# Statistics, scaling, delta pieces and softplus at other places in the queues, and the small scan kept in PSUM

## What is computed

```python
x = x + mamba(cond_scan(x))     # _L0_attn_ref(_L0_cond_ref(x, ...), ...)
x = x + bitlinear_ffn(lowrank_layer(x, cond))
```

## Time and profile before

| | |
|---|---|
| median of 3 runs | 2885.6 us (2884.72 to 2888.72) |
| the profiled execution | 2885.02 us, span 2883.0 us |
| PE busy, DVE busy | 2396.6 us, 2378.5 us |
| ACT busy, POOL busy | 1675.9 us, 1682.5 us |
| mean granted TensorE clock | 0.916 of full speed |
| first and last large scan start | 114.0 us, 2359.3 us |

### The profile page before, as it was taken

How to read it: one execution, slowest core, us unless ns; L and a number is a source line. 1 busy time by engine, 2 the same in 40 slices (tenths; PEclk the granted TensorE clock), 3 DMA queues, 4 the chain that set the end, 5 groups by cost and what they waited for, 6 DMA issues and landing times. The chain is left out here.

```text
span 2883.0 us, 38176 instructions
## 1 busy us (share of the span) xinstructions
PE 2396.6 (83%) x11520; PEld 1642.8 (57%) x11520; DVE 2378.5 (83%) x2438; ACT 1675.9 (58%) x3282; POOL 1682.5 (58%) x1993
## 2 busy tenths in 40 slices
PE   7878878788878888888888888888888794899997
PEld 5556656565656565666665666565656331444443
DVE  2489898898898988898888898898989664688887
ACT  2565656565757565657575656565656444555654
POOL 0266667676767676767676767676767550222221
PEclk8888999998999898999999999999988896999999
DMA  4101010201020201010110101010102531121110
GB/s 171 66 2 68 7 70 5 71 5 70 5 71 5 74 13 63 16 59 31 45 51 24 60 16 60 15 63 13 60 8 89 205 139 71 55 66 55 65 59 23
DMA packets 47510, 152.50 MB, mean 53 GB/s; under 512 B 7973, under 2 KB 8869, under 8 KB 44206
## 3 DMA queue, kind: packets, MB, share of 16 engines
q1 hardware_dynamic: 47278, 149.76, 14.4%
HBM read 132.37 MB, written 17.37 MB: 52 GB/s over the span
## 5 line engine op out<-in xcount | busy, mean ns | idle before, releaser
L451 POOL TENSOR_TENSOR ring<-ring,Cbc 128x512 f32<-128x512 f32 x1024 | 1292.1, 1283 | 44.2
L841 DVE TENSOR_TENSOR_SCAN ring<-a_ps,ring 128x1024 f32<-128x1024 f32 x512 | 1165.2, 2278 | 50.8 <-ACT a_ps L658 50.4
L658 ACT ACTIVATE a_ps<-delta,nA 128x255 f32<-128x255 f32 x2048 | 851.0, 465 | 452.7 <-DVE ring L841 450.5
L1038 PE MATMUL yT_ps<-ident,ring 128*128 128x128 f32 x4096 | 606.4, 291 | 234.4 <-POOL ring L451 224.3
L1038 PEld LDWEIGHTS yT_ps<-ident,ring 128*128 128x128 f32 x4096 | 486.5, 148 | 360.2 <-POOL ring L451 315.2
L833 DVE TENSOR_TENSOR ring<-u_ps,Bbc 128x1024 f32<-128x1024 f32 x512 | 619.9, 1211 | 45.0 <-PE yT_ps L1038 38.9
L1004 PE MATMUL work<-xb,big 128*128 128x256 f32 x2048 | 487.0, 394 | 0.0
L444 POOL TENSOR_TENSOR carry<-ring,half 128x4 f32<-128x4 f32 x512 | 146.5, 286 | 581.7 <-DVE ring L841 579.3
L1004 PEld LDWEIGHTS work<-xb,big 128*128 128x128 f32 x2048 | 398.7, 200 | 54.3 <-issue 0.4
L977 PE MATMUL work<-y0s,big 128*128 128x256 f32 x1024 | 243.6, 396 | 0.7 <-issue 0.7
L1020 PE MATMUL work<-Wout,xb 128*128 128x512 f32 x512 | 239.5, 606 | 0.0
(11 more groups left out here) (194 smaller groups left out, 2697.4 us busy)
## 6 DMA issues: line engine op xcount, KB each, us to landing
Bbc<-bc_rows SPq DMA_DIRECT2D x64, 512.0 KB, 4.5
Cbc<-bc_rows SPq DMA_DIRECT2D x64, 512.0 KB, 3.9
xT<-in_xT SPq DMA_DIRECT2D x16, 514.0 KB, 3.3
x_rows<-x2row SPq DMA_DIRECT2D x32, 256.0 KB, 2.0
xp<-x_rows SPq DMA_DIRECT2D x32, 256.0 KB, 2.7
xx<-in_x SPq DMA_DIRECT2D x32, 256.0 KB, 3.0
out_rows<-orow SPq DMA_DIRECT2D x32, 256.0 KB, 2.0
delta<-in_c_w SPq DMA_DIRECT2D x6, 1024.0 KB, 4.9
```

Source lines behind the costliest of these rows:

```text
L451: nc.gpsimd.tensor_tensor(hp, hp, Cbc[:, G * g + GP * c:G * g + GP * c + GP, :], ALU.mult)\
L658: r = nc.scalar.activation(a_ps[q % 2][:, i, 1:T], delta[:, par, dt, 1:T], ACT.Exp, scale=nA[:, dt, s:s + 1])
L841: dve.tensor_tensor_scan(ring[:, q % RING, :, :].rearrange("p g t -> p (g t)"), a_ps[q % 2][:, :, :].rearrange("p g t -> p (g t)"), ring[: ...
L1038: r = pe.matmul(yT_ps[:, tt, :], ring[:, q % RING, i, P * tt:P * tt + P], ident[:, :], is_transpose=True, start=False, stop=(g == NG - 1 a ...
```

## The change

On DVE, the small scan writes its result over its input in PSUM (bank 0) and no longer to st0; the carry and y0 are read from there. The bank is released one step later: after y0, by a memset that waits for it. A new semaphore, s_sc0, takes the place of the bank's own for the wait on the scan. On DVE the statistics 0 go from slot 7 to 6, the late minimum from slot 4 to 3, the late maximum from slot 6 to 7. On ACT, y0's scaling and copy back, the copies of x and z, zsilu, dexp and dln and the first-column exponential get other slots. On PE, WO1 goes from slot 8 to slot 6, x and z each go about a slot later, and the last two quarters of delta's projection are spread over slots 24 to 31. Nothing is left out and nothing added but the semaphore and the memset.

```diff
@@ -180,6 +180,7 @@
         s_tanh = sem("s_tanh")
         s_l0 = sem("s_l0")
         s_c0 = sem("s_c0")
+        s_sc0 = sem("s_sc0")
         s_y0k = sem("s_y0k")
         s_stat = sem("s_stat")
         s_rstd = sem("s_rstd")
@@ -609,19 +610,19 @@
                     nc.scalar.activation(xw[:, c % 2, :], work[0][0:2, :], ACT.Copy).then_inc(s_rowcp, 1)
 
 
-                next_plan = {5: [prj], 6: [prj_ln], 10: [y0scale], 11: [y0back], 14: [lambda: xcopy(0)],
-                             15: [lambda: xcopy(1)], 16: [lambda: xcopy(2)], 17: [lambda: xcopy(3), silu],
-                             18: [lambda: zcopy(0), lambda: zcopy(1)], 19: [lambda: zcopy(2), lambda: zcopy(3)],
-                             21: [zsilu], 22: [bc], 24: [lambda: dexp(0, False)], 25: [lambda: dexp(1, False)],
-                             26: [lambda: dln(0, False)], 32: [lambda: dexp(2, False)]}
-                scan_plan = {3: [lambda: dexp(3, True)], 6: [lambda: dln(1, True)]}
-                turned = {13: 0, 20: 1, 28: 2}
+                next_plan = {5: [prj], 6: [prj_ln], 12: [y0scale], 13: [y0back], 15: [lambda: xcopy(0)],
+                             16: [lambda: xcopy(1)], 17: [lambda: xcopy(2)], 18: [lambda: xcopy(3), silu],
+                             19: [lambda: zcopy(0)], 20: [lambda: zcopy(1), lambda: zcopy(2)], 21: [lambda: zcopy(3)],
+                             22: [bc], 23: [zsilu], 24: [lambda: dexp(0, False)], 26: [lambda: dexp(1, False)],
+                             27: [lambda: dln(0, False)], 30: [lambda: dexp(2, False)]}
+                scan_plan = {1: [lambda: dexp(3, True)], 6: [lambda: dln(1, True)]}
+                turned = {14: 0, 21: 1, 28: 2}
                 back_plan = {6: [lambda: gT(ND // 2 - 1, fp)], 9: [lambda: wout(0)], 11: [lambda: wout(1)]}
                 for q in range(NQ + 1):
                     dt, g = q // NG, q % NG
-                    if scan and q == FIRST[1] + 2:
+                    if scan and q == FIRST[1] + 3:
                         first_exp(1, k)
-                    if front and q == FIRST[0] + 2:
+                    if front and q == FIRST[0] + 3:
                         first_exp(0, k + 1)
                     if isinstance(k, int) and k == -1 and q == 13:
                         mz_copy()
@@ -717,13 +718,15 @@
                     dve.scalar_tensor_tensor(ps[0:N0, T:2 * T], ps[0:N0, T:2 * T], V[0:N0, V_BS:V_BS + 1], e0[:, :],
                                              ALU.add, ALU.mult).then_inc(s_c0, 1)
                     dve.wait_ge(s_c0, base + 3)
-                    dve.tensor_tensor_scan(st0[:, :], sc0[0:N0, 3:4].to_broadcast([N0, T]), ps[0:N0, T:2 * T],
-                                           carry0[:, fp:fp + 1], ALU.mult, ALU.add).then_inc(free[BANK["PRJ"]], 1)
-                    dve.wait_ge(free[BANK["PRJ"]], jobs_before("PRJ", k) + 1)
-                    dve.tensor_copy(carry0[:, fp:fp + 1], st0[:, T - 1:T]).then_inc(s_c0, 1)
-
-                    dve.scalar_tensor_tensor(y0[0:N0, :], st0[:, :], sc0[0:N0, 1:2], c0[:, :],
+                    dve.tensor_tensor_scan(ps[0:N0, T:2 * T], sc0[0:N0, 3:4].to_broadcast([N0, T]), ps[0:N0, T:2 * T],
+                                           carry0[:, fp:fp + 1], ALU.mult, ALU.add).then_inc(s_sc0, 1)
+                    dve.wait_ge(s_sc0, n + 1)
+                    dve.tensor_copy(carry0[:, fp:fp + 1], ps[0:N0, 2 * T - 1:2 * T]).then_inc(s_c0, 1)
+
+                    dve.scalar_tensor_tensor(y0[0:N0, :], ps[0:N0, T:2 * T], sc0[0:N0, 1:2], c0[:, :],
                                              ALU.mult, ALU.mult).then_inc(s_c0, 1)
+                    dve.wait_ge(s_c0, base + 5)
+                    dve.memset(mark[:, :], 0.0).then_inc(free[BANK["PRJ"]], 1)
 
                 def keep_y0():
 
@@ -843,9 +846,9 @@
                                            ring[:, q % RING, :, :].rearrange("p g t -> p (g t)"), 0.0,
                                            ALU.mult, ALU.add).then_inc(s_scan, 1)
 
-                next_plan = {4: [gates0], 5: [scan0], 7: [lambda: stats(0)], 8: [lambda: stats(1), stats_end],
+                next_plan = {4: [gates0], 5: [scan0], 6: [lambda: stats(0)], 8: [lambda: stats(1), stats_end],
                              13: [keep_y0], 25: [lambda: dmin(0, False)], 27: [lambda: dmax(0, False)]}
-                scan_plan = {4: [lambda: dmin(1, True)], 6: [lambda: dmax(1, True)]}
+                scan_plan = {3: [lambda: dmin(1, True)], 7: [lambda: dmax(1, True)]}
                 for q in range(NQ):
                     if isinstance(k, int) and k == -1 and q == 12:
                         mx_scale()
@@ -1084,18 +1087,18 @@
 
                 plan = {0: [("n", prj, 0), ("n", prj, 1)], 1: [("n", prj, 2)],
                         3: [("b", turn_gated, ND // 2 - 1, k - 1)], 4: [("b", wout, 0, 0)],
-                        5: [("n", wo, 0), ("b", wout, 0, 1)], 6: [("b", wout, 0, 2)],
-                        7: [("b", wout, 1, 0)], 8: [("n", wo, 1), ("b", wout, 1, 1)],
-                        9: [("b", wout, 1, 2), ("n", turn_y0)], 10: [("n", turn_back)],
-                        11: [("s", turn_gated, 0, k), ("n", x, 0, 0), ("n", x, 0, 1)],
-                        12: [("n", x, 1, 0), ("n", x, 1, 1)], 13: [("n", x, 2, 0), ("n", x, 2, 1)],
-                        14: [("n", x, 3, 0), ("n", x, 3, 1)], 15: [("n", z, 0), ("n", z, 1)], 16: [("n", z, 2)],
-                        17: [("n", z, 3)], 18: [("s", turn_gated, 1, k)], 19: [("n", bc)],
+                        5: [("n", wo, 0), ("b", wout, 0, 1)], 6: [("b", wout, 0, 2), ("n", wo, 1)],
+                        7: [("b", wout, 1, 0)], 8: [("b", wout, 1, 1)],
+                        9: [("n", turn_y0), ("b", wout, 1, 2)], 10: [("n", turn_back)],
+                        11: [("s", turn_gated, 0, k)], 12: [("n", x, 0, 0), ("n", x, 0, 1)],
+                        13: [("n", x, 1, 0), ("n", x, 1, 1)], 14: [("n", x, 2, 0), ("n", x, 2, 1)],
+                        15: [("n", x, 3, 0), ("n", x, 3, 1)], 16: [("n", z, 0), ("n", z, 1)], 17: [("n", z, 2)],
+                        18: [("n", z, 3), ("s", turn_gated, 1, k)], 19: [("n", bc)],
                         20: [("n", dl, 0, 0), ("n", dl, 0, 1)], 21: [("n", dl, 0, 2), ("n", dl, 0, 3)],
                         22: [("n", dl, 1, 0), ("n", dl, 1, 1)], 23: [("n", dl, 1, 2), ("n", dl, 1, 3)],
-                        26: [("s", turn_gated, 2, k), ("n", dl, 2, 0)], 27: [("n", dl, 2, 1)],
-                        28: [("n", dl, 2, 2), ("n", dl, 2, 3)], 29: [("n", dl, 3, 0)],
-                        30: [("n", dl, 3, 1), ("n", dl, 3, 2)], 31: [("n", dl, 3, 3)]}
+                        24: [("n", dl, 2, 0)], 25: [("n", dl, 2, 1)],
+                        26: [("s", turn_gated, 2, k), ("n", dl, 2, 2)], 27: [("n", dl, 2, 3)],
+                        28: [("n", dl, 3, 0)], 29: [("n", dl, 3, 1)], 30: [("n", dl, 3, 2)], 31: [("n", dl, 3, 3)]}
                 if isinstance(k, int) and k == 0:
 
                     pe.wait_ge(s_w[6], 16)
```

## The result

The changed kernel took 2854.3 us (median), the kernel before 2886.0 in the same session: 0.9888 of it, 95% interval 0.9872 to 0.9904. So it is 32 us faster, 1.1%, where 68 were forecast; the range ended at 2853. One of its four executions took 3503.7 us at a mean granted clock of 0.64, is a slow one and is left out of the ratio. Its profiled execution took 2850.96 us, span 2848.9.

The account below looks back on a forecast made before the run. DVE was taken to set the pace, except slots 12 to 25, set by PE and ACT. Gains of 1.8 + 1.6 + 0.9 = 4.3 us a block, times 15, plus 4 at the start, make 68: 2817 us, range 2778 to 2853.

Parts of the forecast that it names:

- the first stretch's parts: Slots 0 to 11, DVE sets the end: statistics -4.9, y0 -0.65, late maximum -0.96, late minimum +0.5, sum -6.0 us.
- The hole at L738: DVE's wait for WO1 at the second statistics goes once WO1 stands in slot 6: 4.9 us a block.
- So the 6.0 of the first stretch has shrunk to 1.8: Slots 12 to 25, PE and ACT set the end: DL1 full at +104.4 where it was +106.2.
- rival A: The first stretch's gain is all given back, DL1 at +106.2 as before: 2843 us, chance 0.15.
- half a chance of 1.0: x on PE, slots 12 to 15: lower clock may cost 1.0 us, half counted, so XB3 full at +68.8, not +68.3.
- the third stretch: Slots 26 to 31 and the turn of the block, DVE sets the pace again: gains of 1.6 and 0.9 us.
- the logarithm: ACT's first logarithm goes behind exponentials 26, so DVE's wait of 1.58 us there goes: -1.6 us a block.
- the turn of the block: The last delta products start in slot 24, none doubled up, so DVE's 0.98 us wait goes: -0.9 us.
- the start: Before the first block, WO1 ahead of make_m lets x start some 4 us sooner: 4 us gained once.
- C: Slots 18 to 23, a ring through ACT's z copies, turns and L833 closes four times: slower, 2905 us, chance 0.08.
- The waits foreseen for slots 16 to 24: DVE waits for PE's turns at slots 16, 17, 20, 21, 23, 24 and for ACT at slot 18; no total size given.
- The rule cited from the Trainium skill: A PSUM source adds 62 cycles, making y0 some 0.06 us slower; the forecast rejected it, taking 0.8 faster.

Follow-up runs that it names:

- after_x11: The changed kernel with x, z, the gated copies, ACT's copies and zsilu at their old places, z's copies in pairs: 2798.1 us.
- warm_x: The changed kernel with six extra matmuls a block in PE's idle time ahead of x, written to x's bank before x: 2831.0 us.
- stats_only: The kernel before with only WO1 and statistics 0 moved to slot 6 and the late maximum to slot 7: 2826.5 us.
- xz_as_before: The kernel before with PSUM scan, statistics and late delta pieces; y0's scaling and copy back, x, z, zsilu, first exponential, late minimum at old places: 2787.7 us.
- first_exp_early2: The changed kernel with the first column's exponential two slots behind the column's start, as before, not three: 2850.1 us.
- after_z_pairs2: The changed kernel with ACT's copies of z in pairs again, 0 and 1 in slot 19, 2 and 3 in slot 20: 2871.5 us.
- psum_only: The kernel before with only the small scan kept in PSUM, y0 reading it there and the bank released after y0: 2876.2 us.

## Why the forecast missed

**Right: the first stretch's parts.** The hole at L738 is gone, y0 takes 467 ns (0.48 forecast), L815's successor L818 takes 0.43 in slot 7, and L714 waits 0.58 for ACT in 14 of 14 inner blocks (0.5 forecast). The sum was 6.0 and 5.1 came. 0.5 of the difference is in the trace: DVE's L751, an add over two columns behind the statistics, takes 705 ns in the mean where it took 169 as L748. Before, POOL stood idle while DVE waited at the statistics; now it runs beside them. Block 5, the kernel before first:

```profile
856.73 0.17 DVE L748 TENSOR_SCALAR nrm<-mv 128x2 f32<-128x2 f32 x1
```
```profile
837.46 2.51 POOL L452 TENSOR_TENSOR ring<-ring,Cbc 128x512 f32<-128x512 f32 x2
838.01 0.75 DVE L751 TENSOR_SCALAR nrm<-mv 128x2 f32<-128x2 f32 x1
```

**Right in kind, wrong in size: "So the 6.0 of the first stretch has shrunk to 1.8".** This is the step that failed; what came is 0.3 by the medians of DL1 and -0.3 by the means, so nothing. That is rival A, which had 2.5 us a block and had been given 0.15 (2.3 came in the inner blocks). x(0) came at +53.2 for +52.4: scan 11 ended 0.3 later than in my walk (+49.4), x started 3.4 behind it where I had 3.3, and 3.8 in the six inner blocks in which the turns ahead of x ran at the lower clock. Then x itself ran in part at the lower clock, for which I had 0.5 (half a chance of 1.0) and which cost its first 32 records 0.8 in the mean and 1.7 in block 5 (8.76 against 7.08); x 3 was done 1.1 late. z and bc added 0.5 (+84.6 for +83.0; in the mean 1.1). after_x11 shows that this hangs on the places of x, z and what is tied to them (56 us), and warm_x that 23 us can be had back by the clock alone.

The mechanism itself was in the forecast ("x starts no earlier"). What I did not ask is what the kernel would do with x left in slot 11. stats_only and xz_as_before answer it: it would keep most of the gain: in xz_as_before DL1 is full 4.7 earlier than before.

**Right: the third stretch.** From DL1 on the forecast had 1.6 for the logarithm and 0.9 at the turn of the block. In the means of the inner blocks scan 27 starts 1.4 earlier than before where DL1 was 0.3 later, so 1.7, and the block ends 2.3 shorter, so 0.9 more.

**Wrong: the start.** Forecast 4 us gained, measured 2.1 lost. WO1 ahead of make_m did let x start sooner, but by 1.4 us and not by 4 (60.36 for 61.73: each turn of M takes 1.09 us and then waits 0.29 for a copy on ACT). These 1.4 are lost again before bc starts (83.71 for 83.79), as z's second half takes 3.78 us for 2.53, more of it at the lower clock (78 to 90 us: 0.57 for 0.72). And I had looked at the first exponential's move only inside a block. In step -1 no scan holds ACT back, so the exponential, now in slot 31, stands behind dexp 2 in slot 30, which waits for PE; from L765 to the first scan it is 11.0 us for 8.8 before, 2.2 more. The timeline of DVE in the changed kernel and in first_exp_early2:

```profile
113.43 0.16 DVE L829 TENSOR_REDUCE Bbc<-big 128x4 f32<-128x4 f32 x1 [3.80 <-POOL big L406]
```
```profile
105.60 0.16 DVE L829 TENSOR_REDUCE Bbc<-big 128x4 f32<-128x4 f32 x1 [1.49 <-POOL big L406]
```

**The sum again.** 15 blocks are 36.9 us shorter (2.46 each in the mean, 4.9 of it in the first), less 2.1 at the start and 0.8 in the last block is 34.0; the spans differ by 34.1. The forecast's 68 was 28 too much in the blocks (1.8 each), 6 at the start and 1 in the last block.

**The rivals.** C (a ring through ACT's single copies of z) was wrong beyond its size: after_z_pairs2 shows that these copies cost nothing. Its sum was also off by itself: with DL1 at +112 a block would be 112 - 104.4 - 4.3 = 3.3 longer than before; the 1.6 that gave 2905 fits its +110.4 (1.7). The waits foreseen for slots 16 to 24 came at the slots named but for 20, those of 16 and 24 as large as before (0.64 and 0.62), and at two others: slot 15 (1.8 in the mean, up to 3.1, for 1.0 before) and slot 19 (2.0 in the mean). That these too are for turns that PE did behind x and z, the view says of slot 19; for slot 15 it follows from the times of block 5. The rule cited from the Trainium skill (VectorE: DVE Perf Modes, the TRN2 errata), by which a PSUM source makes a Vector instruction slower, again finds no support: y0 with its PSUM source takes 467 ns, no more than the 0.47 with SBUF sources in the earlier trace rows, and psum_only gained 9.6 us where the rule has a loss.

## What to carry to other kernels

When a wait is taken out of one engine's queue, look for the next job whose place in another queue ties it to a scan or a turn, and ask whether it could now stand earlier; a job moved a slot later "because there is room" can cost more than the wait it makes room for. Where a queue alternates between engines, try each move alone: here three parts give 98 us, and the further moves take 66 of them back, though one of them (y0's turns ahead of WOUT1's last part) is worth 26 by itself. Compare the means of the blocks and not only their medians, and blocks at the same granted clock. Trace an edit through the first pass of a loop as well as the steady one, since what holds an engine back in the one is missing in the other.

## What was not expected of the hardware

PE's granted clock followed what filled its gaps: six extra matmuls a block in idle time raised it in x from 0.79 to 1.00 (by block) to 1.00 throughout and made the kernel 23 us faster. And short DVE instructions are not short beside a busy POOL: the add over two columns takes 169 ns when POOL stands still and 733 to 750 in the 15 blocks in which it doesn't, and the u of slot 7 takes 1.39 us at one place in the queue and 0.43 at another. The trace shows what they end with: in all 15 blocks the add is done 22 to 26 ns behind the end of the POOL multiply (L452, 1.27 us) that was running when it began, and y0 before the change 272 to 281 ns behind the end of such a multiply. All of these have their inputs in SBUF. In the one case in which an input moved to PSUM, y0, the wait is gone.
